# Token parity moved from the inner to the outer place in the columns of a small MLP's operands

## The reference, cut to what matters

```
feat = jnp.concatenate([gath.transpose(0, 1, 3, 2).reshape(NB, n, K * c), st], axis=-1)
h = jax.nn.relu(feat @ W1 + b1)                       # 448 -> 448
rec = (h @ W2 + b2).reshape(NB, n, OC, LH, LW)        # 448 -> 7 * 64
grid = rec.reshape(LRF, LRF, n, OC, LH, LW).transpose(2, 3, 0, 4, 1, 5)
grid = grid.reshape(n, OC, H, W)
return jnp.einsum('bohw,co->bchw', grid, out_w)       # 7 -> 64 channels
```

## Time and profile before

| | |
|---|---|
| median of 3 runs | 761.55 us (759.54 to 763.1) |
| the profiled execution's own time | 760.08 us |
| its span in the trace | 758.3 us |
| mean granted clock of TensorE | 0.95 |
| `second_layer`, four times | 25.9 us of TensorE busy |
| last addition on VectorE ends, from the span's start | 751.5 us |

### The profile page before, as it was taken

How to read it: one execution, slowest core, us unless ns; L and a number is a source line. 1 busy time by engine, 2 the same in 40 slices (tenths; PEclk the granted TensorE clock), 3 DMA queues, 4 the chain that set the end, 5 groups by cost and what they waited for, 6 DMA issues and landing times. The chain is left out here.

```text
span 758.3 us, 25224 instructions
## 1 busy us (share of the span) xinstructions
PE 654.2 (86%) x10662; PEld 373.8 (49%) x10662; DVE 505.2 (67%) x980; ACT 477.6 (63%) x906; POOL 356.1 (47%) x441
## 2 busy tenths in 40 slices
PE   3785689999999999999999759999999988749993
PEld 2663355555555555555545423233333336638883
DVE  4697577877778787777787541377777787361333
ACT  3655266777877778787777537877877754524221
POOL 4588356787777778877777630011212222240000
PEclk9996599999999999999999968999999999969997
DMA  9560000000000000000000010021122211030446
GB/s 211 134 148 12 1 3 3 3 3 2 3 3 3 3 3 3 2 3 3 4 3 2 3 37 21 0 56 46 40 56 56 57 44 45 3 94 3 112 125 209
DMA packets 13112, 29.59 MB, mean 39 GB/s; under 512 B 3457, under 2 KB 4614, under 8 KB 12998
## 3 DMA queue, kind: packets, MB, share of 16 engines
q1 hardware_dynamic: 11874, 27.53, 14.0%
q0 software_dynamic: 272, 0.27, 0.2%
q10 hardware_dynamic: 856, 0.20, 0.1%
HBM read 19.53 MB, written 8.45 MB: 37 GB/s over the span
## 5 line engine op out<-in xcount | busy, mean ns | idle before, releaser
L794 POOL TENSOR_TENSOR sc<-sc,mx 128x512 f32<-128x512 f32 x128 | 132.5, 1044 | 97.1 <-DVE mx L725 97.0
L722 DVE TENSOR_TENSOR sc<-s_ps,bias_tab 128x512 f32<-128x512 f32 x128 | 87.7, 685 | 41.8 <-PE s_ps L528 41.8
L1396 POOL TENSOR_TENSOR square<-xs 128x1024 f32<-128x1024 f32 x16 | 33.8, 2112 | 167.0 <-DVE xs L1165 167.0
L656 ACT ACTIVATE pt<-t_ps 128x512 f32<-128x512 f32 x128 | 75.8, 592 | 36.2 <-PE t_ps L539 35.6
L539 PE MATMUL t_ps<-consts,sc 128*128 128x128 f32 x512 | 84.4, 288 | 15.9 <-ACT pt L656 12.5
L539 PEld LDWEIGHTS t_ps<-consts,sc 128*128 128x128 f32 x512 | 54.2, 142 | 84.5 <-POOL sc L794 43.1
L725 DVE TENSOR_REDUCE mx<-sc 128x8 f32<-128x512 f32 x128 | 87.8, 686 | 4.4
L1080 ACT ACTIVATE hs<-h_ps,fb1s 128x512 f32<-128x512 f32 x128 | 78.3, 689 | 19.1 <-PE h_ps L989 19.0
L528 PE MATMUL s_ps<-kx,qu 32*64 32x128 f32 x2048 | 72.6, 279 | 3.5 <-DVE kx L749 2.9
L989 PE MATMUL h_ps<-xs,fw 64*128 64x512 f32 x256 | 68.7, 650 | 1.0 <-ACT hs L1080 1.0
L528 PEld LDWEIGHTS s_ps<-kx,qu 32*64 32x64 f32 x2048 | 56.9, 134 | 14.4 <-issue 13.3
(11 more groups left out here) (212 smaller groups left out, 1296.3 us busy)
## 6 DMA issues: line engine op xcount, KB each, us to landing
raw<-in_x_dram SPq DMA_DIRECT2D x32, 256.0 KB, 4.8
xr<-in_x_dram SPq DMA_DIRECT2D x32, 256.0 KB, 3.9
out_dram<-x SPq DMA_DIRECT2D x32, 256.0 KB, 3.8
w<-in_L_conv_W_dram SPq DMA_DIRECT2D x1, 784.0 KB
w<-in_L_conv_W_dram SPq DMA_DIRECT2D x1, 672.0 KB
consts<-in_c_consts_dram SPq DMA_DIRECT2D x1, 400.0 KB, 3.8
w1s<-in_L_conv_W_dram SPq DMA_DIRECT2D x2, 112.0 KB
mask<-in_c_mask_dram POOLq DMA_DIRECT2D x1, 128.0 KB, 9.2
```

Of the source, the lines that this page charges most:

```text
L656: act.activation(pt[a][2 * hp + j][:, :, :], t_ps[:, :, :], ACT.Exp).then_inc(s["exped"], 1)
L722: dve.tensor_tensor(sc[n % KEPT][:, :, :, :], s_ps[j][:, :, :, :], bias_tab[:, j, hp], ALU.add)\
L794: pool.tensor_tensor(v, v, mx[n % KEPT][:, :].unsqueeze(2).broadcast_to([128, 8, TOK]), ALU.subtract)\
```

## The change

The columns of a part are put in the order (b, a, q, g): the parity first. For this `feat` and `st_t` get other shapes, and the copies that fill them write to other places. `second_layer` then takes 64 neighbouring columns as its moving operand. Its output columns come in the order (a, q, g) in place of (a, g, q), and `take_rec` becomes two copies, one for each a, with an order of its own. No instruction is moved to another place or another engine.

```diff
-        st_t = sb(whole, "st_t", [128, 2, 256])
+        st_t = sb(whole, "st_t", [128, QUARTERS, 2, 2, 32])
...
-            feat = sb(stage, "feat", [128, TOP // 2, 2, 256])
+            feat = sb(stage, "feat", [128, TOP // 2, QUARTERS, 2, 2, 32])
...
                 for q, (q_lo, q_hi) in enumerate(HALVES):
-                    last = copy(feat[q_lo:q_hi, :, a, 32 * n:32 * (n + 1)].rearrange("c s (m b) -> c m b s", b=2),
-                                src[:, :, :, :, q, a])
+                    at = slice(16 * (n % 2), 16 * (n % 2 + 1))
+                    last = copy(feat[q_lo:q_hi, :, n // 2, :, a, at].rearrange("c s b m -> c m b s"), src[:, :, :, :, q, a])
...
                     for b, (lo, hi) in enumerate(HALVES):
-                        last = dve.tensor_copy(st_t[lo:hi].rearrange("c a (n b) -> c a n b", b=2)[:, :, :, b],
-                                               psb[2][lo:hi, 0:256].rearrange("c (n a) -> c a n", a=2))
+                        last = dve.tensor_copy(st_t[lo:hi, :, b],
+                                               psb[2][lo:hi, 0:256].rearrange("c (k n a) -> c k a n", k=QUARTERS, a=2))
...
-                        copy(rec[:, :, :, 0:2 * OC].rearrange("c g q (a o) -> c o a (g q)", a=2),
-                             psb[1][:, 0:OUTDIM].rearrange("c (o a n) -> c o a n", o=OC, a=2)).then_inc(s["rec"], 1)
+                        for a in range(2):
+                            last = copy(rec[:, :, :, OC * a:OC * (a + 1)].rearrange("c g q o -> c o q g"),
+                                        psb[1][:, 0:OUTDIM].rearrange("c (o a q g) -> c a o q g", o=OC, a=2, q=4)[:, a])
+                        last.then_inc(s["rec"], 1)
...
                             for j in range(TOP // 2):
-                                pe.matmul(hidden_bank(m), w1[:, j, cols], feat[:, j, :, quarter(k)], start=(j == 0), stop=False)
-                            last = pe.matmul(hidden_bank(m), w1s[:, cols], st_t[:, :, quarter(k)], start=False, stop=True)
+                                pe.matmul(hidden_bank(m), w1[:, j, cols], feat[:, j, k].rearrange("c b a n -> c (b a n)"), start=(j == 0), stop=False)
+                            last = pe.matmul(hidden_bank(m), w1s[:, cols], st_t[:, k].rearrange("c b a n -> c (b a n)"), start=False, stop=True)
...
                                 for b, (lo, hi) in enumerate(HALVES):
                                     last = pe.matmul(psb[1][lo:hi, at], w2[:, m, at],
-                                                     hid[:, k % 2, m].rearrange("h (a q g b) -> h b a g q", a=2, q=4, b=2)[:, b],
+                                                     hid[:, k % 2, m, C * b:C * (b + 1)],
                                                      start=(m == 0), stop=(m == 3))
```

More of the change, by code:

```diff
@@ L1507, in spread_feat @@
                 for q, (q_lo, q_hi) in enumerate(HALVES):
-                    last = copy(feat[q_lo:q_hi, :, a, 32 * n:32 * (n + 1)].rearrange("c s (m b) -> c m b s", b=2),
-                                src[:, :, :, :, q, a])
-                return last
-            def quarter(k):
-                return slice(C * k, C * (k + 1))
+                    at = slice(16 * (n % 2), 16 * (n % 2 + 1))
+                    last = copy(feat[q_lo:q_hi, :, n // 2, :, a, at].rearrange("c s b m -> c m b s"), src[:, :, :, :, q, a])
+                return last
             def hidden_bank(m):
@@ L1547, in _ @@
                     pool.memset(ow[:, :], 0.0).then_inc(tail_zero, 1)
-                    pool.memset(st_t[:, :, :], 0.0)
+                    pool.memset(st_t[:, :, :, :, :], 0.0)
                     pool.memset(rec[:, :, :, :], 0.0)
```

## The result

The changed kernel takes 748.78 us (median of 4 runs, 747.77 to 749.76), the kernel before in the same comparison 762.17 (759.54 to 763.1). The ratio is 0.983, 95% interval 0.980 to 0.9859: 1.7% faster. The forecast was 749.5, the range 747.0 to 754.5. The profiled execution took 747.77 us, its span 746.0, against 760.08 and 758.3 before: 12.3 us less, where 12.0 were forecast. Of these, 0.3 us came ahead of the part that was changed: the first `second_layer` starts at 689.46 us of the chain, before at 689.74. That is no gain of the change.

What follows compares the result with a forecast made beforehand. TensorE was taken as the bound, with four second_layer runs on the chain of waits. Saving 3.01 us in each, 12.0 in all, with other terms hidden or absorbed, gave 761.55 - 12.0 = 749.5 us, range 747 to 754.5.

Steps and rivals of the forecast that it cites:

- The pace of the spread columns: In second_layer, spread moving columns stream at half pace or less; a round falls from 111.6 to 57.9 ns, saving 12.0 us.
- First rival, loading sets the pace and nothing changes: In second_layer, weight loads cannot lie beside the stream, so time stays at 761.5 us; 12 in 100.
- Second rival, loading becomes the bound: In second_layer, weight loads hold a round at 64.8 ns, so the gain is 10.5 us, time 751.0; 9 in 100.
- `take_rec`, 0.17 us more: On ScalarE, two rec copies of 224 elements take 1.13 us, 0.17 more than the one copy.
- The stores absorb a delay of `turn_rec(3)`: In part 3, the stores set the end, so the 0.17 us delay of turn_rec(3) does not show.
- the third rival: At the end, backlogged stores lose part 3's gain, up to 3.0 us, time 752.5; 8 in 100.
- The covers: Work ahead of turn_rec hides a late rec copy: 0.28 us in part 0, 0.77 in part 1, 1.9 in part 2.

Runs made afterwards that it cites:

- experiment 1: Changed kernel with the 64 columns still in one block but streamed in the old order, 8 elements apart, and the old single take_rec copy: 761.44 us.
- experiment 3: Changed kernel with second_layer's moving columns at step 4, 16, 3, or in neighbour pairs 16 apart: 763.41, 762.28, 762.36, 749.85 us.
- experiment 5: Changed kernel with the moving operand of 12 of first_layer's 16 matmuls a part taken 16 elements apart: 758.59 us.
- experiment 2: Kernel before, old layout kept, with second_layer streaming its columns at a plain step of 2 and two take_rec copies: 748.54 us.
- experiment 4: Changed kernel with second_layer's moving columns in neighbour pairs that lie across a 16-byte border: 760.79 us.
- experiment 6: Two variants of the changed kernel's second_layer: 32 moving columns in place of 64, 745.30 us; W2's columns taken 7 elements apart, 760.18 us.
- experiment 8: Changed kernel with take_rec first making two extra copies into an unread spare tile, so that rec is ready later: 749.45 us.
- experiment 7: Changed kernel with second_layer summing over two of the four hidden slices, 28 matmuls in place of 56: 744.78 us.

## Why the prediction was right

*The pace of the spread columns* was the step on which all hung, and it held: the same matmuls at 58.7 ns a round (2 x (3.48 - 0.222) / 111) where 57.9 was put, in the middle of L557's 55.9 and L488's 59.8. A part gave 3.0 us as forecast. Experiments 1, 3 and 5 show the cause that was only argued then. Two things were less right than the number. The prediction blamed "the step of two to 64 elements"; experiments 2 and 4 show that a step of two costs nothing and neighbours across a line's border cost everything, so it is the move to another line. And 57.9 ns was taken as a pace of the stream, where the loads of weights hold the 58.7 (experiment 6): that the two lie so near is luck in the reasoning, though the rows of like matmuls that gave the number were the right ones to go by.

*First rival, loading sets the pace and nothing changes:* fell with the result. L557's pace, which spoke against it, was the right row to trust.

*Second rival, loading becomes the bound:* half right. Loading did become the bound (experiment 6), but at 58.7 ns and not at the 64.8 that doubling L1193's 32.4 gave; a proportional rule from 32 to 64 columns overstates it. By these two figures 32 more columns cost 26.3 ns, 0.82 ns each, and some 6 ns are fixed: an estimate from two points.

*The rule of the Trainium skill* (SBUF — State Buffer, "Door 1: The DMA port swizzle") names the right unit, the 16-byte line, and says that at least two hits in a row on a line are needed; experiments 3 and 4 agree, with 3.48 us for two hits and 6.73 for one. Its corollary, that a step of four float32 is free, is not what was measured: step 4 costs 6.73 us, the full price. The Trainium skill's rule on loads (TensorE: Matmul & The Clock Gate, "Part 3: Packing small matmuls — row/col tiling") would have kept the time at 761.5; the trace after does not agree, with 58.7 ns a round and all rows in use, and neither does experiment 6, where half the stream takes off only 0.02 us.

*`take_rec`, 0.17 us more:* wrong, it is nothing. ScalarE's groups by form after the change:

```profile
L1618 ACT ACTIVATE rec<-bank 128x224 f32<-128x224 f32 x8 | 3.8, 576 | 13.4 <-PE bank L1749 13.4
```

A copy takes 576 ns as worked out (565), but two take 0.94 us, not 1.15: the second starts 0.2 us ahead of the first one's end. I had added two lengths.

*The stores absorb a delay of `turn_rec(3)`:* wrong for a delay of 0.8 us, and without effect on the sum, since `take_rec` cost nothing. Experiment 8 shows that the end follows `turn_rec(3)`; for the 0.17 us of the prediction no run tells. That the stores could still follow held, and the third rival with its 752.5 us fell: all of part 3's gain is there at the end. The next limit that experiment 7 shows is VectorE's additions, not the stores.

*The covers:* the prediction gave part 0 only 0.28 us to hide a late `rec`. Experiment 8 made it later by 0.8 us, and part 0 lost nothing.

*What was not foreseen* is 0.36 us given back ahead of the last addition. The timeline of the kernel before has this for the start of `add(3, 0)`:

```profile
746.63 1.29 DVE L1612 TENSOR_TENSOR x<-x,bank 128x512 f32<-128x512 f32 x2 [0.84 <-PE grid_ps L1779]
```

So it came 746.63 - 743.21 = 3.42 us after `turn_rec(3)` had started, and now comes 734.67 - 730.89 = 3.78 after. The windows show where, first of the changed kernel (the last three figures of a row are the granted clock, the DMA share and GB/s), then of the kernel before:

```profile
730.00:732.00 2.00, 1.98 (x24) 1.35 (x20) 1.01 (x2) 0.84 (x2) 0.00 (x0) 1.00 0.81 240
732.00:734.00 2.00, 0.91 (x16) 0.83 (x19) 1.47 (x3) 1.02 (x1) 0.00 (x0) 0.93 0.78 221
734.00:736.00 2.00, 2.00 (x24) 1.45 (x16) 1.32 (x3) 0.00 (x0) 0.00 (x0) 0.50 0.97 259
```
```profile
748.00:750.00 2.00, 0.00 (x0) 0.00 (x0) 2.00 (x4) 0.00 (x0) 0.00 (x0) 1.00 0.90 293
750.00:752.00 2.00, 0.00 (x0) 0.00 (x0) 1.50 (x3) 0.00 (x0) 0.00 (x0) 0.54 0.81 241
```

The granted clock fell from 2.4 to 1.2 GHz between 732 and 734 us, with `mix(3, 0)` under way; before, it fell only behind 750 us, when TensorE had no work left. In the window in which it fell TensorE was busy for 0.91 of 2.00 us. The kernel of experiment 8 has 0.63 in the window 732 to 736, and pays 4.36 us where 3.42 was. But this is no fixed price of the change. With half the second layer left out (experiment 7) the clock fell at about 701 us and was back at 1.00 when the last matmuls ran. And experiment 1, as slow as the kernel before, has the fall among its last matmuls too: the 16 records of `mix(3, 1)` take 1.91 us there and took 1.04 in the kernel before.

```profile
744.78 1.91 PE L1775 MATMUL bank<-xs,ow 14*128 14x256 f32 x16
```
```profile
746.38 1.04 PE L1779 MATMUL bank<-xs,ow 14*128 14x256 f32 x16
```

Where the clock falls differs from trace to trace, and no run here tells why.

The medians differ by 13.4 us, the profiled executions by 12.3. The medians of the kernel before, each of several runs, ranged from 760.7 to 762.2 beside the kernels of this document, so I make nothing of the 1.1 us.

## What to carry to other kernels

Before a layout is changed for a TensorE operand, count how often its reading moves to another 16-byte line from one column to the next. Neither the step, nor the neighbours, nor the number of lines touched in all will do. Two float32 columns in a row from one line were enough here; one from each line cost double for the moving operand, and in the one spread order that was run, a step of 7, for the stationary one. A cheaper change may lie in another order of reading over the same layout; here the plain step of 2 in the old layout gave the same time. And a record that lasts longer than those of its kind with the same number of columns (289 ns against 219) shows a loss before anything is built, but not in which operand: with spread weights it was 281.

## What the runs showed of the hardware

- Lines: a round of two 64-column tiles takes 115.9 ns when the reading moves to another 16-byte line 64 times and 86.7 when 48 times, 1.81 ns a move; with 32 moves (pairs in a line) it is 58.8, as with neighbours, and there the weight loads seem to hold it.
- The same 64 columns in the same 16 lines take 3.48 us a part when read in order and 6.62 when read 8 apart.
- The step of 16 was a little cheaper than that of 4 and of 8: 6.40 us a part against 6.73 and 6.62. Why is open; no run tells.
- Two tiles of 64 columns on all 128 rows run at 58.7 ns a round, and 32 in place of 64 moving columns save 0.02 us of 3.48, so the stream lies beside what holds the round.
- Two ScalarE copies in a row overlap by some 0.2 us (2 x 0.576 against 0.94) when they write scattered elements.
